# Projection blocks two chunks deep, with exchanged copies taken from the PSUM banks

## The chip, the cores and the metric

The kernel runs on one core of one Trainium2 chip. The metric is the device time of one execution in microseconds (us). A difference of under about 0.2% (6.5 us) can't be told from no change. The engines are called PE (matmul), DVE (vector), ACT (scalar), POOL (GpSimd) and SP (which issues most DMAs).

## The reference

`x` has 4 images of 32 x 32 tokens with 192 channels (4096 tokens). Cut to what matters here, the reference is

```python
x = x + conv_attention(layer_norm(x))     # L0: q, k, v = y @ qkv_w.T + qkv_b, 12 heads of 16
t = t + routed_experts(layer_norm(t))     # 8 experts, top 2
x = x + conv_attention(layer_norm(x))     # L1
h = ln1(layer_norm(t)) ; t = t + attention(h) ; t = t + mlp(t) ; t = t + experts(ln2(t))
```

Each `conv_attention` adds to its scores a bias of relative positions, `einsum(q, Rh)` over rows and `einsum(q, Rw)` over columns. All three attentions begin with the same work: normalize the tokens, then project them to q, k and v with a bias vector.

## The kernel before

`build` (line 2328) runs stages one after the other. The function `front` (line 196) is the projection block. It runs three times: as **c0** (with `load`, it also loads the tokens), as **c1** (with `back`, it first adds the rows that the experts left in DRAM) and as **f1** (with `hidden`, a layer norm within a layer norm, and without relative positions). After each comes `attention` (line 735), which starts when all stores of q, k and of the position bias have landed.

`front` treats the 4096 tokens as 8 chunks of 512 (4 tiles of 128 tokens). Every product is done in float16 with a high and a low part of each operand, so that the sum is close to float32. For one chunk the work is this:

- DVE takes statistics (`prepare`, line 481: in c1 first eight additions at line 491; `bn_stats` at line 506; `spread`, lines 450 to 459), ACT takes the square root (`root`, line 607), and DVE finishes mean and factor (`settle`, lines 466 to 476). c0 and f1 do this for 8 tiles at once, that is in every second chunk; c1 for 4.
- The chunk is normalized into `nrm` (2 buffers): by DVE in c0 (line 521), by ACT in c1 and f1 (line 619).
- PE turns it (`turn_over`, lines 365 and 366) into the banks t0 and t1. ACT writes the high parts (`high_parts`, line 625) and DVE the low parts (`low_parts`, lines 530 and 531). t0 and t1 exist once, so the next `turn_over` waits for `low_parts`.
- PE projects: `turned(c, g)` for g = 0, 1, 2 gives q and k of four heads (6 products of 512 columns, lines 377 to 382, the last is the bias as a product of `cl` with ones) and `values(t)` for four tiles gives v (5 products of 192 columns, lines 389 to 393). Both have three banks in turn (`qp`, `vp`).
- ACT reads a bank into `high` (`high_of`, line 638), then DVE writes `low` (line 540) and, having read `vp` with the bias `bv` added, `vt` (line 543); both stand in `take`.
- SP stores q and k (line 272) once DVE has written `low` for an image and group; in f1 POOL stores the keys.
- In c0 and c1, ACT copies q of a chunk, high and low, with rows and columns of the image exchanged, into `by_x` (`by_column`, line 648): six copies of 64 x 512 float16, one chunk late, read from SBUF with a step of 16 elements. The last chunk's six copies come after the loop.

Each engine has its own order, written out by hand. Before, step c is this, and chunk c-1's projection and chunk c's turning stand in the same step:

```python
for c in range(CHUNKS + 1):               # DVE
    if c: take(c - 1)
    if c < CHUNKS: low_parts(c)
    if c + 1 < CHUNKS: prepare(c + 1); finish(c + 1)
```

PE does `turned(c-1, 0..1)`, `values`, `turn_over(c)`, `turned(c-1, 2)`, `values`. After the chunks, in c0 and c1, PE multiplies q with the tables of positions (lines 435 to 440: 48 units of a bank, 12 products of 128 columns each where k is 0, 8 where k is 1), ACT and DVE drain high and low parts (lines 693 and 597), and ACT and SP store them (line 278). ACT stores a set of eight units while it drains the next set.

In c1 POOL gathers the experts' rows (line 328), eight indirect DMAs a chunk, into four ring buffers.

Of the kernel before, what the change touches and what calls it, by code (L numbers as in the profile page):

```python
# [16 lines left out]
F16 = mybir.dt.float16  # L17
# [7 lines left out]
T = B * L  # L25
# [170 lines left out]
def front(nc, name, src, eps, stats, parts, ident, vt, w, scratch, kept, spare=None, load=None, back=None, hidden=None):  # L196
# [10 lines left out]
    by_act = load is None  # L207
# [3 lines left out]
    with Pool(nc, name) as m:  # L211
# [13 lines left out]
        raw_c, ch, cl = m.sb("rawc", 2 * C, parts=64), m.sb("ch", 2 * C, F16, parts=64), m.sb("cl", 2 * C, F16, parts=64)  # L225
        ones = m.sb("ones", CHUNK, F16, parts=64)
        bv = m.sb("bv", C)
# [8 lines left out]
        s_zero, s_w, s_b, s_tab = m.sem("zero"), m.sem("w"), m.sem("b"), m.sem("tab")  # L236
# [8 lines left out]
        s_byx = m.sem("byx")  # L245
# [8 lines left out]
        by_x = parts  # L254

# [4 lines left out]
        def by_rows(t, c, g):  # L260

            return t[0:GW, at(c, g)].rearrange("p (s y x) -> p s x y", s=2, y=QSIDE)
# [19 lines left out]
        with nc.Block() as block:  # L282
            @block.sync
            def _(sp):
# [13 lines left out]
                sp.dma_start(raw_c[:, :], w["bqk"]).then_inc(s_w, 16)  # L298
                sp.dma_start(bv[:, :], w["bv"].broadcast_to([P, C])).then_inc(s_b, 16)
# [58 lines left out]
            def _(pe):  # L358
# [10 lines left out]
                def turned(c, g):  # L369
# [14 lines left out]
                def values(t):  # L384
# [8 lines left out]
                    pe.matmul(bank, xb[:, tokens], bl[:, 2 * C:W], start=False, stop=True).then_inc(s_v, 1)  # L393
# [3 lines left out]
                for c in range(CHUNKS + 1):  # L397
                    if c == 1:
# [3 lines left out]
                    if c:  # L402
                        for g in range(2):
                            turned(c - 1, g)
                            values(TC * (c - 1) + g)
                    if c < CHUNKS:
                        turn_over(c)
                    if c:
                        turned(c - 1, 2)
                        for j in range(2, TC):  # L410
                            values(TC * (c - 1) + j)
# [7 lines left out]
                for g in range(GROUPS):  # L419
                    top, rest = high[:, g * T:(g + 1) * T], low[:, g * T:(g + 1) * T]  # L420
                    for k in range(2):
                        if k and g == 0:
                            pe.wait_ge(s_byx, 2 * CHUNKS * GROUPS)
# [20 lines left out]
            def _(dve):  # L444
# [65 lines left out]
                def finish(c):  # L510

                    if TC * c % SET == 0:
                        settle(TC * c, SET, mean, rstd, TC * c // SET + sets)
                    if by_act:
                        return
                    dve.wait_ge(s_rstd, 5 * (TC * c // SET + sets + 1))
                    if c >= 2:
                        dve.wait_ge(s_turned, c - 1)
                    for j in range(TC):
                        t = TC * c + j  # L520
                        dve.tensor_scalar(nrm[c % 2][:, j * C:(j + 1) * C], src[:, ts(t, C)], mean[:, t:t + 1],
                                          rstd[:, t:t + 1], ALU.subtract, ALU.mult).then_inc(s_norm, 1)
# [10 lines left out]
                def take(c):  # L533
                    for j in range(TC):
                        t = TC * c + j
                        b, kt = t // KT, t % KT
                        if j < GROUPS:
                            n, cols = c * GROUPS + j, at(c, j)
                            dve.wait_ge(s_hi, n + 1)
                            dve.scalar_tensor_tensor(out=low[:, cols], in0=qp[n % 3][:, :], scalar=1.0 / W_SCALE,  # L540
                                                     in1=high[:, cols], op0=ALU.mult, op1=ALU.subtract).then_inc(s_lo, 1)
                        dve.wait_ge(s_v, t + 1)
                        dve.scalar_tensor_tensor(out=vt4[:, NH // 2 * b:NH // 2 * (b + 1), kt, :],
                                                 in0=vp[t % 3][:, 0:C].rearrange("p (g f) -> p g f", f=2 * HD),
                                                 scalar=1.0 / W_SCALE,
                                                 in1=bv[:, :].rearrange("p (g f) -> p g f", f=2 * HD),
                                                 op0=ALU.mult, op1=ALU.add).then_inc(s_vt, 1)

                def queries_of(t):
                    return t[:, 0:2 * C].rearrange("p (g s f) -> p g s f", g=GROUPS, s=2)[:, :, 0, :]  # L550

# [4 lines left out]
                else:  # L556
                    if load:
                        prepare(0)
                dve.wait_ge(s_w, 7 * 16)
                for t in (raw_a, raw_b, raw_c):  # L560
                    dve.tensor_scalar(queries_of(t), queries_of(t), float(HD) ** -0.5, None, ALU.mult).then_inc(s_q, 1)
                if not load:
                    prepare(0)
                finish(0)
                dve.wait_ge(s_wh, 4)
                for n, (raws, tops, lows) in enumerate(((raw_a[:, :], ah[:, :], al[:, :]),
                                                        (raw_b[0:C1, :], bh[0:C1, :], bl[0:C1, :]),
                                                        (raw_c[32:64, :], ch[32:64, :], cl[32:64, :]))):
                    dve.scalar_tensor_tensor(out=lows, in0=raws, scalar=W_SCALE, in1=tops, op0=ALU.mult,
                                             op1=ALU.subtract).then_inc(s_wl, 1)  # L570
                dve.wait_ge(s_b, 16)
                for c in range(CHUNKS + 1):
                    if c:
                        take(c - 1)
                    if c < CHUNKS:
                        low_parts(c)
                    if c + 1 < CHUNKS:
                        prepare(c + 1)
                        finish(c + 1)
# [21 lines left out]
            def _(act):  # L601
# [7 lines left out]
                def normalize(c):  # L609
                    if TC * c % SET == 0:  # L610
                        root(TC * c, SET, TC * c // SET + sets)
                    if not by_act:
                        return
# [21 lines left out]
                def high_of(c, g):  # L635
# [3 lines left out]
                                   scale=1.0 / W_SCALE).then_inc(s_hi, 1)  # L639

                def by_column(c):

                    act.wait_ge(s_v, TC * (c + 1))
                    act.wait_ge(s_lo, GROUPS * (c + 1))
                    act.wait_ge(s_hi, GROUPS * (c + 1))
                    for g in range(GROUPS):
                        for rows, buf in ((slice(0, GW), high), (slice(GW, P), low)):
# [5 lines left out]
                if load:  # L653
                    root(0, SET, 0)
# [5 lines left out]
                if not load:  # L660
                    normalize(0)
# [1812 lines left out]
```

## Time and profile before

| | |
|---|---|
| median of 3 runs (lowest to highest) | 3267.11 us (3266.5 to 3270.53) |
| profiled execution: device time, span | 3268.62 us, 3266.5 us |
| PE, PEld, DVE, ACT, POOL busy | 81%, 37%, 73%, 59%, 14% of the span |
| mean granted PE clock | 0.90 of full (2.4 GHz) |
| c0: first projection product to first bias product | 24.8 to 114.1 us |
| c1: the same | 1128.5 to 1236.4 us |
| f1: first projection product to last value read | 1925.0 to 2034.1 us |

Read it so: the device time is the span plus some 2 us at its ends. Busy shares are means over stages with different limits. The three projection phases take 306 us of the 3266.5, and it is within them that the change acts. A granted clock of 0.5 is the lower level (1.2 GHz), 1.0 the upper (2.4 GHz); a mean between them is time spent at either.

### The profile page before, as it was taken

The numbers are of one execution on the slowest core, as the hardware profiler recorded it, in microseconds if no ns is written. First come the engines' busy times: TensorE is split into PE (matmuls) and PEld (weight loads), VectorE is DVE, ScalarE is ACT, GpSimd is POOL, SyncE is SP. The second block draws the span as 40 slices with busy tenths as digits, with TensorE's granted clock in tenths as the row PEclk, the third lists the DMA queues.
The fourth block names the chain that finished last, engine by engine and source line by source line (L and its number), as shares of the span: only waits on it lengthen the run. The fifth ranks groups of instructions, "written<-read, shape, count | busy, mean of one in ns | idle before, by whom it ended". The sixth has DMA issues, their size and how long they took to land. (4 is left out here: it accounts for less than half of the span.)

```text
span 3266.5 us, 62245 instructions
## 1 busy us (share of the span) xinstructions
PE 2633.6 (81%) x18588; PEld 1197.2 (37%) x18588; DVE 2399.4 (73%) x4681; ACT 1937.5 (59%) x2701; POOL 455.1 (14%) x542
## 2 busy tenths in 40 slices
PE   5648999997499575599999956488888859599998
PEld 2502222225499434122222233011111336266666
DVE  5578999984665565799999654799999644565565
ACT  5716777773255476277777733177777734564654
POOL 0010111111333440101111101101112100000000
PEclk9859999997599877699999977599999979699999
DMA  2475776663122236656766512112222100200000
GB/s 84 155 152 105 150 149 142 144 143 119 55 76 78 74 101 187 117 124 147 149 146 145 109 39 58 34 52 58 64 60 63 47 22 1 73 6 5 10 9 11
DMA packets 209761, 282.39 MB, mean 86 GB/s; under 512 B 57934, under 2 KB 101886, under 8 KB 209610
## 3 DMA queue, kind: packets, MB, share of 16 engines
q1 hardware_dynamic: 166250, 213.15, 28.7%
q0 software_dynamic: 23696, 34.77, 4.5%
q10 hardware_dynamic: 19664, 32.60, 3.3%
q8 instruction: 77, 1.26, 0.2%
q14 instruction: 74, 0.61, 0.1%
HBM read 201.94 MB, written 77.46 MB: 86 GB/s over the span
## 5 line engine op out<-in xcount | busy, mean ns | idle before, releaser
L988 DVE TENSOR_REDUCE c0att_mx<-c0att_m 128x1 f32<-128x512 f32 x768 | 493.3, 685 | 35.0 <-PE c0att_m L925 29.3
L988 DVE TENSOR_REDUCE c1att_mx<-c1att_m 128x1 f32<-128x512 f32 x768 | 493.3, 685 | 34.8 <-PE c1att_m L925 29.6
L988 DVE TENSOR_REDUCE f1att_mx<-f1att_m 128x1 f32<-128x512 f32 x768 | 480.1, 682 | 21.3 <-PE f1att_m L925 19.3
L1263 ACT ACTIVATE c0att_p<-c0att_s 128x1024 f32<-128x1024 f32 x384 | 373.9, 1020 | 151.7 <-PE c0att_s L941 151.6
L1263 ACT ACTIVATE c1att_p<-c1att_s 128x1024 f32<-128x1024 f32 x384 | 373.9, 1020 | 150.9 <-PE c1att_s L941 150.7
L1263 ACT ACTIVATE f1att_p<-f1att_s 128x1024 f32<-128x1024 f32 x384 | 373.3, 1020 | 121.3 <-PE f1att_s L941 121.3
L925 PE MATMUL f1att_m<-f1att_km,f1att_qm 48*128 48x512 f16 x768 | 156.3, 403 | 130.9 <-DVE f1att_mx L988 99.4
L1694 ACT ACTIVATE moe_h<-moe_u,moe_bu 128x512 f32<-128x512 f32 x192 | 136.7, 712 | 177.0 <-PE moe_u L1611 95.1
L925 PE MATMUL c0att_m<-c0att_km,c0att_qm 64*128 64x512 f16 x768 | 156.4, 403 | 64.6 <-DVE c0att_mx L988 36.2
L925 PE MATMUL c1att_m<-c1att_km,c1att_qm 64*128 64x512 f16 x768 | 156.3, 403 | 62.8 <-DVE c1att_mx L988 35.0
L954 PE MATMUL c1att_o<-c1att_p,c1att_vs 128*32 128x512 f32 x1536 | 206.1, 609 | 0.6 <-ACT c1att_p L1263 0.6
L954 PE MATMUL c0att_o<-c0att_p,c0att_vs 128*32 128x512 f32 x1536 | 206.0, 608 | 0.6 <-ACT c0att_p L1263 0.6
L954 PE MATMUL f1att_o<-f1att_p,f1att_vs 128*32 128x512 f32 x1536 | 205.8, 608 | 0.7 <-ACT f1att_p L1263 0.5
L1624 PE MATMUL moe_y<-moe_dh,xt 128*128 128x192 f16 x1536 | 195.5, 246 | 0.0
L1731 DVE TENSOR_TENSOR xt<-moe_h,xt 128x512 f16<-128x512 f32 x192 | 131.3, 691 | 86.5 <-ACT xt L1696 85.6
L1624 PE MATMUL moe_y<-moe_dl,xt 128*128 128x192 f16 x768 | 189.1, 246 | 0.0
L925 PEld LDWEIGHTS f1att_m<-f1att_km,f1att_qm 48*128 48x128 f16 x768 | 38.1, 93 | 371.2 <-DVE f1att_mx L988 335.1
L925 PEld LDWEIGHTS c0att_m<-c0att_km,c0att_qm 64*128 64x128 f16 x768 | 37.9, 93 | 298.6 <-DVE c0att_mx L988 265.4
L925 PEld LDWEIGHTS c1att_m<-c1att_km,c1att_qm 64*128 64x128 f16 x768 | 37.8, 93 | 297.1 <-DVE c1att_mx L988 264.8
L941 PE MATMUL c0att_s<-xt,c0att_ka 113*128 113x512 f16 x512 | 136.5, 389 | 7.1 <-DMA xt<-c0att_mrow 6.6
L941 PE MATMUL c1att_s<-xt,c1att_ka 113*128 113x512 f16 x512 | 136.5, 389 | 6.9 <-DMA xt<-c1att_mrow 6.3
L1624 PEld LDWEIGHTS moe_y<-moe_dh,xt 128*128 128x128 f16 x1536 | 139.2, 98 | 3.8 <-issue 0.3
(623 smaller groups left out, 5326.3 us busy)
## 6 DMA issues: line engine op xcount, KB each, us to landing
xt<-rel_parts SPq DMA_DIRECT2D x256, 128.0 KB, 5.0
xt<-qk_parts SPq DMA_DIRECT2D x192, 128.0 KB, 4.4
y<-rel_parts SPq DMA_DIRECT2D x128, 128.0 KB, 5.8
y<-qk_parts SPq DMA_DIRECT2D x96, 128.0 KB, 5.3
c0att_qm<-rel_parts SPq DMA_DIRECT2D x144, 64.0 KB, 2.1
c1att_qm<-rel_parts SPq DMA_DIRECT2D x144, 64.0 KB, 2.1
f1att_ka<-qk_parts SPq DMA_DIRECT2D x144, 64.0 KB, 2.1
expert_rows<-y SPq DMA_DIRECT2D x39, 192.0 KB, 2.0
```

Source lines behind the costliest of these rows:

```text
L925: ins = pe.matmul(bank[:, :], qm[v][rows, q0:q0 + P], km[v][rows, c * CHUNK:(c + 1) * CHUNK], start=True, stop=True)
L941: ins = pe.matmul(sps[h][:, c * CHUNK:(c + 1) * CHUNK], ka[u][rows, kcol], qa[u][rows, queries(h, version, c * CHUNK, CHUNK)], start=True, ...
L954: ins = pe.matmul(ops[row:row + 32, :], vs[u][:, (h * KT + kt) * 32:(h * KT + kt + 1) * 32], pr[h][kt % 2][:, c * CHUNK:(c + 1) * CHUNK], ...
L988: dve.tensor_reduce(mx[:, n:n + 1], bank[:, :], AX.X, ALU.max).then_inc(s_mx, 1)
L1263: act.activation(pr[h][kt % 2][:, :], sps[h][:, :], ACT.Exp).then_inc(s_e, 1)
L1624: ins = pe.matmul(yps[q % 2][t // 2][:, (t % 2) * C:(t % 2 + 1) * C], hidden[q % 2][:, x], down[:, w], start=k == 0 and i == 0, stop=k == ...
L1694: act.activation(h32[:, i % 2 * CHUNK:(i % 2 + 1) * CHUNK], bank[:, :], ACT.Gelu, bias=bias, scale=1.0 / W_SCALE).then_inc(s_h32, 1)
L1731: dve.tensor_tensor(hl[q % 2][:, cols], h32[:, i * CHUNK:(i + 1) * CHUNK], hh[q % 2][:, cols], ALU.subtract).then_inc(s_hl, 1)
```

## The change

`front` is rewritten in its order and in a few of its operations:

- **Two steps apart.** The loop has 10 steps. In step s DVE prepares chunk s and ACT normalizes it last in the step; chunk s-1 is turned and split into parts; chunk s-2 is projected and read out. The turning stands behind the first unit `turned(c, 0)`.
- **Roots early.** ACT's `root` comes right after `high_parts`; DVE's `settle` comes after the first `low_of`.
- ACT normalizes in c0 too.
- **Exchanged copies from the banks.** The high half of `by_x` is written by ACT straight from the PSUM bank, right after `high`; the low half by DVE from `low`. The copies of a chunk belong to its own step, and none is left behind the loop. `low_of` and the bank's next use now also wait for ACT's exchanged copy.
- **Bias of v as a product.** `cl` and `raw_c` are 576 wide, `values` has a sixth product (64 rows, 192 columns), `bv` and its DMA are gone. v is read out by ACT in c1 and by DVE in c0 and f1.
- The parts of x lie in `xt` (halves) and no longer in `y` (thirds), which `by_x` keeps for itself.

```diff
@@ front, PE @@
                     if n >= 3:
                         pe.wait_ge(s_lo, n - 2)
+                        if rel:
+                            pe.wait_ge(s_byh, n - 2)
...
-                    pe.matmul(bank, xb[:, tokens], bl[:, 2 * C:W], start=False, stop=True).then_inc(s_v, 1)
+                    pe.matmul(bank, xb[:, tokens], bl[:, 2 * C:W], start=False, stop=False)
+                    pe.matmul(bank, ones[:, 0:P], cl[:, 2 * C:W], start=False, stop=True).then_inc(s_v, 1)
...
+                for step in range(1, CHUNKS + 2):
+                    c = step - 2
...
+                    if c >= 0:
+                        turned(c, 0)
+                    if step <= CHUNKS:
+                        turn_over(step - 1)
+                    if c >= 0:
+                        values(TC * c)
+                        for g in range(1, GROUPS):
+                            turned(c, g)
+                            values(TC * c + g)
+                        values(TC * c + GROUPS)
@@ front, DVE @@
+                def exchange(c, g):
+                    if not rel:
+                        return
+                    dve.wait_ge(s_lo, c * GROUPS + g + 1)
+                    dve.tensor_copy(by_columns(by_x[g][GW:P, :], c), by_rows(low, c, g)).then_inc(s_byl, 1)
...
+                if back:
+                    scale_queries()
+                for step in range(CHUNKS + 2):
+                    c = step - 2
+                    if step < CHUNKS:
+                        prepare(step)
+                    if c >= 0:
+                        low_of(c, 0)
+                    if step < CHUNKS:
+                        finish(step)
+                    if c >= 0:
+                        take(TC * c)
+                    if 1 <= step <= CHUNKS:
+                        low_parts(step - 1)
+                    if c >= 0:
+                        exchange(c, 0)
+                        for g in range(1, GROUPS):
+                            low_of(c, g)
+                            take(TC * c + g)
+                            exchange(c, g)
+                        take(TC * c + GROUPS)
+                    if step == 0 and not back:
+                        scale_queries()
+                    if step == 1:
+                        split_low()
@@ front, ACT @@
+                    if rel:
+                        act.activation(by_columns(by_x[g][0:GW, :], c), exchanged(qp[n % 3][0:GW, :]), ACT.Identity,
+                                       scale=1.0 / W_SCALE).then_inc(s_byh, 1)
...
+                for step in range(CHUNKS + 2):
+                    c = step - 2
+                    if c >= 0:
+                        high_of(c, 0)
+                        take(TC * c)
+                    if 1 <= step <= CHUNKS:
+                        high_parts(step - 1)
+                    if step < CHUNKS and TC * step % SET == 0:
+                        root(TC * step, SET, TC * step // SET + sets)
+                    if c >= 0:
+                        high_of(c, 1)
+                        take(TC * c + 1)
+                        high_of(c, 2)
+                    if step < CHUNKS:
+                        normalize(step)
+                    if c >= 0:
+                        for j in range(2, TC):
+                            take(TC * c + j)
...
-                by_column(CHUNKS - 1)
```

## Rows read from the trace of the kernel before

**Rows 1.** Windows: c0, c1, f1 projection phases, then c0's bias drain; columns named first.

```profile
core 0: us, PE busy (x) PEld busy (x) DVE busy (x) ACT busy (x) POOL busy (x), PEclk, DMA share, GB/s
24.80:114.10 89.30, 68.16 (x360) 34.20 (x361) 54.35 (x159) 64.21 (x82) 0.00 (x0) 0.89 0.16 55
1128.50:1236.40 107.90, 75.93 (x361) 36.03 (x362) 73.06 (x235) 77.00 (x114) 45.61 (x47) 0.81 0.29 90
1925.00:2034.50 109.50, 80.30 (x360) 37.46 (x360) 52.34 (x151) 43.76 (x80) 14.30 (x24) 0.75 0.20 48
126.00:170.00 44.00, 27.07 (x384) 23.77 (x384) 31.51 (x48) 27.74 (x48) 0.00 (x0) 0.85 0.84 261
```

**Rows 2.** Waits (us in total, times, longest): c0's projection phase, then f1's.

```profile
DVE c0qkv_low L540 <- ACT c0qkv_high L638: 30.3, 12, 4.8
PE c0qkv_qp L377 <- DVE y L531: 19.1, 8, 2.9
...
DVE f1qkv_low L540 <- ACT f1qkv_high L638: 55.0, 21, 3.6
```

**Rows 3.** Timeline of DVE, one step of c1: start, us, line, operands, idle before.

```profile
1197.60 2.85 DVE L491 SCALAR_TENSOR_TENSOR x<-c1qkv_sent,top,x 128x192 f32<-128x192 f32 x8
1200.48 1.14 DVE L506 BATCH_NORM_STATS2 stats<-x 128x6 f32<-128x192 f32 x4
1201.65 0.17 DVE L450 TENSOR_TENSOR c1qkv_mean<-stats 128x4 f32<-128x4 f32 x1
...
1202.71 0.18 DVE L466 RECIPROCAL c1qkv_rstd<-c1qkv_std 128x4 f32<-128x4 f32 x1 [0.27 <-ACT c1qkv_std L607]
...
1203.51 0.16 DVE L476 SCALAR_TENSOR_TENSOR c1qkv_away<-c1qkv_mean,c1qkv_rstd 128x4 f32<-128x4 f32 x1
...
1208.78 0.69 DVE L540 SCALAR_TENSOR_TENSOR c1qkv_low<-c1qkv_qp,c1qkv_high 128x512 f16<-128x512 f32 x1 [0.88 <-ACT c1qkv_high L638]
1209.38 0.61 DVE L543 SCALAR_TENSOR_TENSOR vt<-c1qkv_vp,c1qkv_bv 128x192 f32<-128x192 f32 x2
1209.91 0.68 DVE L530 TENSOR_TENSOR y<-c1qkv_t,y 128x512 f16<-128x512 f32 x1
```

**Rows 4.** Timeline of PE in c0: one chunk's work, then the bias products.

```profile
30.92 0.27 PE L365 MATMUL c0qkv_t<-ident,c0qkv_sent 128*128 128x128 f32 x1
...
31.80 0.38 PE L377 MATMUL c0qkv_qp<-y,c0qkv_ah 128*128 128x512 f16 x1
...
32.97 0.39 PE L382 MATMUL c0qkv_qp<-c0qkv_ones,c0qkv_cl 64*128 64x512 f16 x1
33.29 0.26 PE L389 MATMUL c0qkv_vp<-c0qkv_ah,y 128*128 128x192 f16 x1
...
33.71 0.25 PE L389 MATMUL c0qkv_vp<-c0qkv_ah,y 128*128 128x192 f16 x1
...
36.61 0.61 PE L377 MATMUL c0qkv_qp<-y,c0qkv_ah 128*128 128x512 f16 x1 [2.32 <-DVE y L531]
...
114.12 0.22 PE L438 MATMUL c0qkv_qp<-c0qkv_high,c0qkv_th 128*128 128x128 f16 x1 [1.60 <-DVE vt L543]
...
114.28 0.22 PE L438 MATMUL c0qkv_qp<-c0qkv_high,c0qkv_th 128*128 128x128 f16 x1
```

**Rows 5.** Timeline of ACT: end of c0's projections; then c1's normalization.

```profile
124.69 1.11 ACT L648 ACTIVATE y<-c0qkv_low 64x512 f16<-64x512 f16 x1
125.82 1.57 ACT L693 ACTIVATE c0qkv_sent<-c0qkv_qp 128x512 f16<-128x512 f32 x3
...
129.89 0.69 ACTq L278 DMA_DIRECT2D rel_parts<-c0qkv_sent  x1
...
1203.70 1.86 ACT L619 ACTIVATE c1qkv_sent<-x,c1qkv_away,c1qkv_rstd 128x192 f32<-128x192 f32 x4 [1.03 <-DVE c1qkv_away L476]
```

**Rows 6.** Timelines of POOL and DVE in c1: last gather, first additions.

```profile
1187.17 0.95 POOL L328 DMA_INDIRECT c1qkv_sent<-expert_rows,give  x1 [0.30 <-issue]
...
1115.74 2.85 DVE L491 SCALAR_TENSOR_TENSOR x<-c1qkv_sent,top,x 128x192 f32<-128x192 f32 x8 [5.02 <-DMA c1qkv_sent<-expert_rows,give]
```

More of the change, by code:

```diff
@@ new lines, in low_of, with take @@
+                def low_of(c, g):
+                    n, cols = c * GROUPS + g, at(c, g)
+                    dve.wait_ge(s_hi, n + 1)
+                    if rel:
+                        dve.wait_ge(s_byh, n + 1)
+                    dve.scalar_tensor_tensor(out=low[:, cols], in0=qp[n % 3][:, :], scalar=1.0 / W_SCALE,
+                                             in1=high[:, cols], op0=ALU.mult, op1=ALU.subtract).then_inc(s_lo, 1)
+                def take(t):
+                    if back:
+                        return
+                    dve.wait_ge(s_v, t + 1)
+                    dve.tensor_scalar(values_to(t), values_from(t), 1.0 / W_SCALE, None, ALU.mult).then_inc(s_vt, 1)
@@ L555, in _ @@
                     dve.wait_ge(s_rstd, 5)
[L556 to L579, printed above, removed]
+                if back:
+                    scale_queries()
[22 more added lines that the diff above has]
+                        split_low()
                     if rel and c == 1:
@@ L639, in high_of @@
                                    scale=1.0 / W_SCALE).then_inc(s_hi, 1)
[L641 to L647, printed above, removed]
-                            act.activation(by_columns(by_x[g][rows, :], c), by_rows(buf, c, g),
-                                           ACT.Identity).then_inc(s_byx, 1)
+                    if rel:
+                        act.activation(by_columns(by_x[g][0:GW, :], c), exchanged(qp[n % 3][0:GW, :]), ACT.Identity,
+                                       scale=1.0 / W_SCALE).then_inc(s_byh, 1)
@@ L651, in _, with take @@
+                def take(t):
+                    if not back:
+                        return
+                    act.wait_ge(s_v, t + 1)
+                    act.activation(values_to(t), values_from(t), ACT.Identity, scale=1.0 / W_SCALE).then_inc(s_vt, 1)
                 if hidden:
                     root(0, TILES, 0)
-                if load:
-                    root(0, SET, 0)
-                act.wait_ge(s_q, 3)
-                act.activation(ah[:, :], raw_a[:, :], ACT.Identity, scale=W_SCALE).then_inc(s_wh, 1)
@@ L657, in _ @@
[L657 to L673 removed]
+                if back:
+                    split_high()
@@ new lines, in _ @@
+                for step in range(CHUNKS + 2):
[16 more added lines that the diff above has]
+                            take(TC * c + j)
+                    if step == 0 and not back:
+                        split_high()
```

113 lines of the change are left out of this document (40 added, 73 removed).

## The prediction

> **What bounds the kernel now.** I looked first at the windows of the three projection phases [rows 1]. In none of them is an engine full: PE is busy 68.2 of 89.3 us in c0, 75.9 of 107.9 in c1, 80.3 of 109.5 in f1; DVE 54.4, 73.1, 52.3; ACT 64.2, 77.0, 43.8. So a chain bounds them. The waits name it [rows 2]: in c0 DVE waits 30.3 us for ACT's `high` and PE 19.1 us for DVE's low parts; in f1 DVE waits 55.0 us. Line 377's first product of a chunk starts after 2.32 us of idleness and then at the lower clock (0.61 us against 0.38) [rows 4]. Chunk c's read-out, chunk c+1's low parts and its projection stand one behind the other, 11.2 us a chunk in c0, 13.5 in c1 and 13.7 in f1 (by eighths) [rows 1]. The granted clock is 0.89, 0.81 and 0.75: part of PE's busy time is the lower level. Last, in c0 the first bias product is at 114.12 [rows 4], but ACT drains its first bank at 125.82, since its exchanged copies still run at 124.69, 1.11 us each [rows 5]. From there DMA is the limit: 261 GB/s and a share of 0.84 in c0's drain [rows 1].
>
> **Prices, start to start.** PE at the upper clock [rows 4]: `turned` 33.29 - 31.80 = 1.49; `values` 33.71 - 33.29 = 0.42; `turn_over` 31.80 - 30.92 = 0.88. DVE [rows 3]: `low` 1209.38 - 1208.78 = 0.60; a v read-out 0.53 / 2 = 0.27; low parts 2 x 0.7 = 1.4; statistics of 4 tiles 1201.65 - 1200.48 = 1.17; additions 2.88; both chains 1203.67 - 1201.65 less the wait for the root of some 0.3, 1.75. ACT: four normalizations 1.86, three drains of a bank 1.57, one exchanged copy from SBUF some 1.13 [rows 5].
>
> **The new operations.** *Sixth product of v.* Line 382 (64 rows) starts 32.97 and line 389 0.32 later, where a 512-column product takes 0.22; the five before it take 31.80 to 32.97, 1.17 for 5 x 0.215. So a change between 128 and 64 rows costs some 0.1 each way, and the product itself 0.08: I take 0.28 for each of 32 tiles, bounds 0.08 and 0.32. A chunk on PE is then 3 x 1.49 + 4 x 0.70 + 0.88 = 8.15 us at the upper clock, before 7.03.
> *ACT's exchanged copy from the bank.* The drains of line 693 read a bank into float16, 0.5 us start to start [rows 5]; half of all 48 units of that line read with a large step, and the mean of all 48 is the same, 27.74 / 48 = 0.58 us of busy time [rows 1]. I take 0.5, bounds 0.5 and 1.15. ACT's work on a c0 chunk is then 3 x (0.5 + 0.5) + 1.0 + 1.8 = 5.8, below DVE's at either bound.
> *DVE's exchanged copy E from SBUF.* No such DVE copy is in the trace. ACT's copy is the same walk of 64 x 512 float16 at a step of 32 bytes, and takes 1.13 where a bank's read takes 0.5 [rows 5]. It is the nearest row: E = 1.15. Bounds: 0.6 (DVE's `low` of as many columns [rows 3]) and 1.7 (half as much again as ACT).
> The Trainium skill (Advanced Engine Details and Errata, SBUF Cachelines) says that accesses landing on a different 16-byte line each time are penalized; by that rule E is well above 0.6, and the trace agrees for ACT. Against the rule, with E at 0.6, the sum below would come out some 11 us lower. Its next section (PSUM Cachelines) makes the same claim of banks, for matmuls; by it ACT's copy would go to the upper bound, which line 693's mean does not bear out.
>
> **c0.** Chunks pipeline, so the busiest engine sets the pace. DVE from the first projection product (24.8, which stays: the weights' splitting leads to it) to the last `low`: 8 x (3 x 0.60 + 4 x 0.27 + 3 x 1.15) = 50.6; low parts of chunks 1 to 7, 9.8; statistics of chunks 2, 4 and 6 (8 tiles each), 3 x (2.34 + 1.75) = 12.3; tables 1.4. Sum 74.1, plus 1.5 in the last step, where DVE follows PE: 100.4. PE alone would need 8 x 8.15 - 0.9 = 64.3, at a granted 0.9 71.4: it fits, barely. 114.1 to 100.4 is **-14**. The normalizations that leave DVE for ACT (1.2 us a chunk) are in this sum.
>
> **c1.** Per chunk DVE has 2.88 + 1.17 + 1.75 + 1.4 + 1.8 + 3.45 = 12.45 (v goes to ACT): eight are 99.6, with the splitting of weights and tables 103. It starts at 1115.74 [rows 6]. Chunk 1's additions now stand ahead of chunk 0's low parts, and its last gather is issued 48 issues of 1.25 us before 1187.17 [rows 6], near 1127, landing near 1128.5, while DVE is through with chunk 0 at 1121.7: 7 us of new idleness. Gathers come every 10 us and are hidden after that. 1115.7 + 103 + 7 + 2 = 1228 for 1236.4: **-8**.
>
> **f1.** DVE has 52.3 / 8 = 6.5 us a chunk, ACT 43.8 / 8 = 5.5 [rows 1], PE 8.15: PE is the bound. I take a granted clock of 0.9, what c0 has now with more gaps: 8 x 8.15 = 65.2, less 0.9 for the first turning, by 0.9 is 71.5 us from 1925.0: 1996.5 for 2034.5, **-38**. What was waiting is gone since the turning, the parts and the products belong to three chunks. POOL's stores of keys follow each `low` as before and stay idle between.
>
> **The tail of c0 and c1.** Twelve copies of 1.15 leave the way. ACT's first store, which opens the DMA-bound part, comes at 129.89 [rows 5], 15.8 us after the first bias product. Now PE gives the pace of the first eight units: three products take 0.16 (114.12 to 114.28) [rows 4], twelve 0.67, eight units 5.4, and one drain: 6.2. **-9.6** in each, **-19** together. The bytes stored are the same, so the end moves with the start. The last chunk's stores of q and k precede the bias stores by some 5 us and are hidden; before they lay beneath the copies.
>
> **At nothing:** the wider `raw_c` and the missing `bv` DMA (in SP's row of weight loads), ACT's v read-outs in c1 (4 x 0.3, ACT has 3 us of slack a chunk), the wait of `low_of` on ACT's copy (0.5 us, DVE has statistics in between).
>
> **Sum** against the profiled execution: 3268.6 - 14 - 8 - 38 - 19 = 3189.6. The median of the runs shown is 1.5 us below that execution, so I say **3189 us** (-2.4%).
>
> **Rivals.**
> *A, all cheap (0.15).* E is 0.6 and PE stays near the upper level. c0 is then PE's, 3 to 5 us less; c1 gains 7 more; f1 at 0.97 4 to 5. 3173. For it: PE's gaps shrink. Against: ACT's 1.13.
> *B, the gain in c0 and c1 is only the tail (0.17).* E is 1.7: 24 x 0.55 = 13.2 us more in each block, c1 even 4 behind before: 3215. Or PE stays at a mean of 0.75, the value of f1 now: 10.9 us a chunk, c0 -2, f1 -23, c1 -5: 3219.
> *C, slower (0.04).* The stretches run mostly at the lower clock. A chunk is 13.6 us at a mean of 0.6: c0 ends at 132, 18 later, c1 9 later, f1 2 earlier, tails -19 + 8 as the first units slow too: 3282. It decides from a mean of about 0.62. Against: PE is idle less often, and the lowest of the three phases has 0.75 [rows 1].
> *D, nothing moves (0.02).* The blocks' ends are set by stores or by the stage's change, not by the projections. Against: the first store follows the drain within 4 us [rows 5], and DMA's share is 0.16 to 0.29 in the projection phases [rows 1].
>
> **Chances.** The forecast has 0.62, with its own range 3177 to 3204. The range 3168 to 3224 adds A and B. Faster by over 0.2% 0.94, the same (within 0.2%, what a measurement of this kernel can't tell from no change) 0.02, slower 0.04.
>
> **What would show it.** Right: c0's first bias product near 100, c1's near 1228 shifted by c0's gain, f1's phase 71 us at a clock near 0.9; DVE's waits for `high` in f1 nearly gone; ACT's first store 6 us after the first bias product; DVE's copy near 1.15. Wrong: a DVE copy of over 1.6 or under 0.7; f1's clock still 0.75; PE waiting in f1 for normalization or for v's banks.

## The result and the profile after

The changed kernel takes **3181.97 us** (median of four runs, 3178.76 to 3185.25) beside 3266.81 for the kernel before, measured with it: ratio **0.974**, 95% interval 0.9723 to 0.9757. The forecast was 3189, the range 3168 to 3224. The profiled execution, the longest of the four, took 3185.25 us, with a span of 3183.2, 83.3 less than before.

Here are windows of the changed kernel, to be read beside [rows 1]: c0's projection phase, then its bias part up to the attention's load of its weights, the same two of c1, and f1 from its first to its last unit of q and k (a unit is one `turned`; PEld is PE's loading of weights).

```profile
core 0: us, PE busy (x) PEld busy (x) DVE busy (x) ACT busy (x) POOL busy (x), PEclk, DMA share, GB/s
26.90:97.90 71.00, 68.18 (x392) 33.90 (x393) 61.08 (x155) 44.83 (x92) 0.00 (x0) 1.00 0.20 71
97.90:153.40 55.50, 32.46 (x480) 28.25 (x480) 32.80 (x48) 28.66 (x48) 0.00 (x0) 0.84 0.81 252
1113.30:1197.50 84.20, 72.54 (x393) 35.75 (x394) 72.97 (x204) 51.56 (x127) 40.33 (x40) 0.89 0.34 104
1197.50:1257.00 59.50, 32.38 (x480) 28.74 (x480) 33.04 (x49) 28.66 (x48) 0.00 (x0) 0.78 0.79 241
1881.50:1947.70 66.20, 64.48 (x374) 32.27 (x374) 49.84 (x146) 43.52 (x78) 12.33 (x20) 0.97 0.31 73
```

In c0 PE does in 71 us what took it 89, and 32 more products; the granted clock is 1.00 instead of 0.89, in f1 0.97 instead of 0.75. ACT's 64 us have become 45.

The waits of the changed kernel in c0's phase (total, times, longest):

```profile
ACT c0qkv_high L651 <- PE c0qkv_qp L388: 20.7, 16, 4.9
...
DVE c0qkv_low L537 <- ACT y L654: 6.3, 10, 1.1
...
PE c0qkv_qp L383 <- DVE xt L530: 0.8, 2, 0.5
```

and in f1's:

```profile
ACT f1qkv_high L651 <- PE f1qkv_qp L388: 20.6, 15, 4.9
...
DVE f1qkv_low L537 <- ACT f1qkv_high L651: 6.2, 7, 1.5
```

The direction has turned [rows 2]. In c0 DVE waited 30.3 us for ACT and PE 19.1 for the low parts; these are 6.3 and 0.8, and it is ACT that waits. In f1 DVE's 55.0 us have become 6.2. The 6.3 us are `low` waiting for ACT's exchanged copy (L654). Not in these rows is a wait of PE of 12.6 us for `cl`, the weights' low part, which ends with the first projection product, here at 26.9.

DVE's timeline in one step of c0, with the new copy (L550) beside `low` (L537) and v's read-out (L544), in the place of [rows 3]:

```profile
35.99 0.69 DVE L537 SCALAR_TENSOR_TENSOR c0qkv_low<-c0qkv_qp,c0qkv_high 128x512 f16<-128x512 f32 x1
36.59 0.35 DVE L544 TENSOR_SCALAR vt<-c0qkv_vp 128x192 f32<-128x192 f32 x1
36.97 0.62 DVE L550 COPY y<-c0qkv_low 64x512 f16<-64x512 f16 x1
37.63 0.69 DVE L537 SCALAR_TENSOR_TENSOR c0qkv_low<-c0qkv_qp,c0qkv_high 128x512 f16<-128x512 f32 x1
```

The copy takes 0.62 us, not 1.15. The sixth product of v is as priced. On PE's timeline of one `values`, its first product, its fifth and sixth (L400) and the next one's first are

```profile
61.48 0.26 PE L395 MATMUL c0qkv_vp<-c0qkv_ah,xt 128*128 128x192 f16 x1
...
61.82 0.25 PE L399 MATMUL c0qkv_vp<-c0qkv_bl,xt 128*128 128x192 f16 x1
62.00 0.25 PE L400 MATMUL c0qkv_vp<-c0qkv_cl,c0qkv_ones 64*128 64x192 f16 x1
62.18 0.26 PE L395 MATMUL c0qkv_vp<-c0qkv_ah,xt 128*128 128x192 f16 x1
```

62.18 - 61.48 = 0.70, against 0.42 before. The tail is what follows the projections: the bias products, their drains and stores. Its start in c0 is on these rows of the changed kernel (first bias product, ACT's first drain, its first store; before 114.12, 125.82 and 129.89 [rows 4, 5]):

```profile
97.91 0.27 PE L447 MATMUL c0qkv_qp<-c0qkv_high,c0qkv_th 128*128 128x128 f16 x1 [2.04 <-DVE vt L544]
...
99.39 0.60 ACT L712 ACTIVATE c0qkv_sent<-c0qkv_qp 128x512 f16<-128x512 f32 x1 [3.82 <-PE c0qkv_qp L449]
...
105.49 0.69 ACTq L283 DMA_DIRECT2D rel_parts<-c0qkv_sent  x1
```

### The profile page after: what moved, and what is told of

The parts are those of the page before. It is cut to its first block and busy times, and to the rows that moved or that the text cites. A ratio compares the mean times of both kernels' runs of the same rounds, so it can differ in the third digit from the quotient of the medians.

```text
span 3183.2 us, 62491 instructions
## 1 busy us (share of the span) xinstructions
PE 2619.3 (82%) x18684; PEld 1194.0 (38%) x18684; DVE 2413.1 (76%) x4665; ACT 1876.8 (59%) x2717; POOL 456.6 (14%) x542
## 5 line engine op out<-in xcount | busy, mean ns | idle before, releaser
L1007 DVE TENSOR_REDUCE c0att_mx<-c0att_m 128x1 f32<-128x512 f32 x768 | 493.4, 685 | 34.8 <-PE c0att_m L944 29.7
L1007 DVE TENSOR_REDUCE c1att_mx<-c1att_m 128x1 f32<-128x512 f32 x768 | 493.4, 685 | 34.1 <-PE c1att_m L944 28.9
```

What stands on the lines that cost most here:

```text
L1007: dve.tensor_reduce(mx[:, n:n + 1], bank[:, :], AX.X, ALU.max).then_inc(s_mx, 1)
```

## The experiments

All kernels are edits of the changed one. They ran on three chips, each beside the kernel before, which took 3266.3 us on the first (copies_late, one_step, copy_twice, five_v), 3264.2 on the second (rows128, both v_on_act, start_up) and 3265.6 on the third (the others). So medians of different chips can be compared to some 3 us. The ratio is the measurement's own and differs by up to 0.0014 from the quotient of two medians of this table. The places come from one profiled execution each, which can lie far from the median of its kernel: 13.6 us above it in v_on_act_rows128, 12.8 in root_late, 7.6 in turn_second, 5.6 in five_v. In the eleven kernels that leave no copies behind the loop the drain, whose bytes are the same, goes from 55.1 to 62.1, so one execution doesn't show a difference of a few us in one place.

The columns are **c0** from the first product of q and k (L383) to the first bias product; **drain** from there to the first load of the attention's projection weights (`c0att_pw`); **c1 block** from the load of c1's weights (`rawa`) to `c1att_pw`; **f1** from the first to the last unit of q and k.

| kernel | us | ratio (95%) | c0 | drain | c1 block | f1 |
|---|---|---|---|---|---|---|
| before | 3266.8 | 1 | 89.3 | 63.7 | 197.1 | 105.6 |
| changed | 3182.0 | 0.974 (.9723-.9757) | 71.0 | 55.5 | 177.8 | 66.2 |
| copies_late | 3266.4 | 1.0002 (.999-1.0014) | 115.1 | 62.4 | 214.7 | 66.1 |
| copies_behind | 3218.1 | 0.9854 (.9838-.9871) | 85.8 | 64.1 | 193.9 | 66.2 |
| one_step | 3281.5 | 1.0051 (1.0034-1.0068) | 108.2 | 55.1 | 199.0 | 104.8 |
| copy_twice | 3194.9 | 0.9794 (.9772-.9817) | 78.1 | 55.4 | 182.7 | 66.5 |
| five_v | 3175.3 | 0.9731 (.9713-.9748) | 70.8 | 56.8 | 178.7 | 65.8 |
| rows128 | 3176.2 | 0.9728 (.9712-.9744) | 67.3 | 57.6 | 178.1 | 64.6 |
| v_on_act | 3176.7 | 0.9729 (.9713-.9745) | 67.6 | 57.6 | 176.5 | 66.9 |
| v_on_act_rows128 | 3172.5 | 0.9716 (.9699-.9732) | 63.4 | 62.1 | 179.2 | 65.0 |
| start_up | 3179.5 | 0.9733 (.9716-.9749) | 71.4 | 56.8 | 180.2 | 65.9 |
| root_late | 3201.2 | 0.9792 (.9772-.9813) | 83.7 | 55.9 | 184.8 | 73.4 |
| turn_second | 3205.1 | 0.9812 (.9795-.9828) | 79.4 | 58.3 | 178.1 | 82.8 |
| straight | 3174.4 | 0.9716 (.97-.9732) | 68.9 | 57.2 | 174.3 | 66.0 |

### Is the miss the size of DVE's copy?

copy_twice:

```diff
                     dve.wait_ge(s_lo, c * GROUPS + g + 1)
+                    dve.tensor_copy(again[GW:P, :].rearrange("p (s x y) -> p s x y", s=2, x=QSIDE), by_rows(low, c, g))
                     dve.tensor_copy(by_columns(by_x[g][GW:P, :], c), by_rows(low, c, g)).then_inc(s_byl, 1)
```

> The changed kernel with DVE's exchanged copy made twice (the second into a buffer of its own), so that the pair costs about the 1.15 us that the prediction gave to one. Theory (the prediction's sum failed only by the size of this copy): DVE then has 61 + 15 = 76 us of work in c0's phase of 71 and 73 + 15 = 88 in c1's of 84; the first bias product of c0 goes from 97.9 to 102 to 106 and c1's phase from 84 to 92 to 98. Together +12 to +22, 3194 to 3204 us, and f1 as it is. Rival (the copies are hidden at either size, the miss has another cause): within 4 us of the changed kernel, 3178 to 3186.

3194.94, 13 us above the changed kernel and clear of noise, with c0 7.1 and c1's block 4.9 longer and f1 as it was: the theory, though c1's phase, at 91.0, stayed just under the 92 to 98. A pair of copies costs 1.23, so with E near 1.15 this kernel would have come within some 6 us of the forecast, from above.

straight:

```diff
-                    dve.tensor_copy(by_columns(by_x[g][GW:P, :], c), by_rows(low, c, g)).then_inc(s_byl, 1)
+                    dve.tensor_copy(by_x[g][GW:P, c * CHUNK:(c + 1) * CHUNK], low[0:GW, at(c, g)]).then_inc(s_byl, 1)
...
-                        act.activation(by_columns(by_x[g][0:GW, :], c), exchanged(qp[n % 3][0:GW, :]), ACT.Identity,
+                        act.activation(by_x[g][0:GW, c * CHUNK:(c + 1) * CHUNK], qp[n % 3][0:GW, :], ACT.Identity,
```

> The changed kernel with the two exchanged copies made straight: DVE's from SBUF and ACT's from the bank read their 512 elements in order, so that half of the bias inputs are in the wrong order and this part of the result is left wrong. It measures what the 32-byte step costs each engine. If the step costs DVE nothing, as its 0.616 us beside the 0.69 of a low from a bank suggest, the straight copy stays at 0.6 and the time within 2 us. If the step does slow DVE (the rule of the Trainium skill, Advanced Engine Details and Errata, SBUF Cachelines, which ACT's 1.11 to 1.13 us bore out), the straight copy is well below, 0.2 to 0.4 us, and c0's phase is 1 to 4 us shorter, c1's 4 to 8: 3170 to 3178 us. ACT's copy from the bank stays at 0.58 by either.

The instructions of the two lines in this kernel (min/median/max ns), DVE's from SBUF, then ACT's from a bank:

```profile
L550 DVE COPY y<-c0qkv_low x24: 277/287/289, 32.9 to 92.9; 64x512 f16<-64x512 f16 x24
```

```profile
L654 ACT ACTIVATE y<-c0qkv_qp x24: 577/578/579, 28.3 to 91.2; 64x512 f16<-64x512 f32 x24
```

and the same two in the changed kernel:

```profile
L550 DVE COPY y<-c0qkv_low x24: 602/617/636, 35.4 to 96.7; 64x512 f16<-64x512 f16 x24
```

```profile
L654 ACT ACTIVATE y<-c0qkv_qp x24: 577/578/579, 30.2 to 95.0; 64x512 f16<-64x512 f32 x24
```

The step makes DVE's copy 2.15 times as long, and costs ACT's read of a bank nothing. The prediction's error was to carry ACT's time over: DVE is slowed too, but from 0.287. The kernel's 3174.4 lies in the range, but its interval still overlaps that of the changed kernel, and c1's phase is 2.2 shorter, where 4 to 8 were expected. The Trainium skill (VectorE: DVE Perf Modes, What auto-detection actually checks) gives DVE its fastest mode only where a single source and the destination lie in SBUF, both 16-bit at a step of one. That the strided copy is the slower one agrees with this; which mode either copy ran in is not shown.

### Does the order need the early copies, or the copies the order?

copies_late:

```diff
+                def by_column(c):
+                    act.wait_ge(s_lo, GROUPS * (c + 1))
+                    act.wait_ge(s_hi, GROUPS * (c + 1))
+                    for g in range(GROUPS):
+                        for rows, buf in ((slice(0, GW), high), (slice(GW, P), low)):
+                            act.activation(by_columns(by_x[g][rows, :], c), by_rows(buf, c, g),
+                                           ACT.Identity).then_inc(s_byh, 1)
...
                         high_of(c, 2)
+                    if rel and c > 0:
+                        by_column(c - 1)
                     if step < CHUNKS:
                         normalize(step)
```

> The changed kernel with its new order, but the exchanged copies as before: all six by ACT from SBUF, one chunk late, the last chunk's behind the projections. Theory (the order needs the cheap copies): ACT then has 3 x 0.5 + 6 x 1.13 + 1.0 + 1.9 = 11.2 us of work in each chunk of c0, more than the 8.7 PE needs, and becomes the bound there: c0's first bias product near 115 instead of 97.9, c1's phase some 14 us longer than 84.1, both tails 8 to 10 us longer; f1, which has no such copies, stays at 69. Together about +50, 3232 us. Rival (the copies only cost the two tails, since ACT hides them in the steps): c0's first bias product stays within 2 us of 97.9, and the time is about +19, 3201 us.

3266.4, 34 us above the theory and not to be told from the kernel before. f1 keeps its whole gain (66.1), and c0 is 26 us longer than before the change, its first bias product at 140.0 where the theory had 115. Its window and its waits in c0's phase:

```profile
24.90:140.00 115.10, 80.75 (x392) 39.42 (x392) 46.79 (x131) 75.36 (x107) 0.00 (x0) 0.82 0.13 42
```

```profile
DVE c0qkv_low L532 <- ACT c0qkv_high L643: 56.2, 21, 9.1
PEld c0qkv_t L369 <- ACT c0qkv_sent L624: 33.4, 5, 6.7
ACT c0qkv_high L643 <- PE c0qkv_qp L386: 32.3, 16, 4.9
PE c0qkv_t L369 <- ACT c0qkv_sent L624: 31.9, 5, 6.4
```

ACT is busy 75 of 115 us, so its work is not the bound. PE's turning waits 31.9 us for the normalization, which stands behind six copies; meanwhile ACT waits 32.3 for PE. They take turns, which neither theory nor rival had.

copies_behind changes only that place:

```diff
-                    if rel and c > 0:
-                        by_column(c - 1)
                     if step < CHUNKS:
                         normalize(step)
+                    if rel and c > 0:
+                        by_column(c - 1)
```

> The kernel of the run copies_late (new order, exchanged copies by ACT from SBUF, one chunk late), with one thing moved: in a step ACT now normalizes ahead of the six copies, not behind them. Theory (what cost 44 us in c0's phase there was not only ACT's work but its place: the copies stood between the last read-out of a chunk and the normalization that PE's turning waits for, so PE and ACT took turns): ACT's work of 11.2 us a chunk remains the bound, c0's phase 88 to 95 instead of 115.1, c1's 98 to 105 instead of 122.8, total 3220 to 3235 us against 3266. Rival (the copies delay ACT's high as well, which frees the banks, so the place does not matter): within 8 us of 3266.

```profile
24.90:110.70 85.80, 74.39 (x393) 36.19 (x394) 46.38 (x131) 74.16 (x106) 0.00 (x0) 0.90 0.17 57
```

3218.1, 48 us faster for two lines swapped, and 2 below the range. c0 is at 85.8, where 88 was the least expected, and ACT (74.2) and PE (74.4, at a granted 0.90) are now busy alike, so that ACT alone is the bound isn't shown. This kernel and the changed one differ by the copies' engine, source and time, and by the waits that belong to them, so early cheap copies are worth 3218.1 - 3182.0 = 36 us in the new order; which of the three counts was not tried. In the profiled executions c0 has 14.8 of it, its drain 8.6 and c1's block 16.1.

one_step:

```diff
+                for c in range(CHUNKS + 1):
+                    if c:
+                        for g in range(GROUPS):
+                            low_of(c - 1, g)
+                            take(TC * (c - 1) + g)
+                            exchange(c - 1, g)
+                        take(TC * (c - 1) + GROUPS)
+                    if c < CHUNKS:
+                        low_parts(c)
+                    if c + 1 < CHUNKS:
+                        prepare(c + 1)
+                        finish(c + 1)
```

(DVE's loop; PE's and ACT's likewise in the order of before, the normalization of c0 left on ACT.)

> The changed kernel with its new copies and the bias product of v, but the order of before: chunk c's read-outs ahead of chunk c+1's low parts on DVE, turning behind the second unit, roots beside the normalization (which stays on ACT in all three blocks, as do c1's v read-outs). Theory (the distance of two steps makes the projection phases, the copies make the tails): f1's phase goes back to about 109 us (+40), c0's to 84 to 89 (+13 to +18), c1's by +8 to +12; the tails stay at 7 to 8 us. Sum +61 to +70, 3243 to 3252 us. Rival (in c0 and c1 it was ACT's copies out of the way that shortened the chain, not the distance): only f1 goes back, 3222 us.

3281.54, 15 us slower than the kernel before, and 30 more than expected. f1 goes back to 104.8: its gain is the order's alone, and the sixth product costs nothing there. The drain stays at 55.1: its gain is the copies' alone. c0's phase is 19 us worse than before, c1's 8 (116.1 for 107.9). The waits in c0's:

```profile
DVE c0qkv_low L536 <- ACT y L647: 42.8, 19, 4.2
ACT c0qkv_high L644 <- PE c0qkv_qp L388: 35.6, 17, 5.2
PE c0qkv_qp L383 <- DVE xt L529: 25.5, 8, 3.7
```

In the old order read-outs, low parts and the next projection are one chain, and every early copy is a link of it: `low` waits for ACT's copy, the low parts stand behind DVE's. So in c0's projection phase the copies alone lose 19 us and the order alone gains 3.5 at best (copies_behind, 85.8 for 89.3), where the two together gain 18. (Part of the 19 may be the normalization that moved to ACT; that wasn't tried alone.)

### Early root, and turning behind the first unit

root_late:

```diff
-                    if step < CHUNKS and TC * step % SET == 0:
-                        root(TC * step, SET, TC * step // SET + sets)
                     if c >= 0:
                         high_of(c, 1)
                         take(TC * c + 1)
                         high_of(c, 2)
+                    if step < CHUNKS and TC * step % SET == 0:
+                        root(TC * step, SET, TC * step // SET + sets)
```

> The changed kernel with one thing undone: ACT takes the root behind the third high of a step, beside the normalization, not behind the high parts. DVE waits for it in the middle of the statistics' chain, in order, with v's read-out, the low parts and the later lows behind it. Theory (the early root is part of what makes the pipeline): DVE waits some 3 to 5 us more in each step with a root, 3 such steps of c0 and f1 and 7 of c1: c0's phase +8 to +15, f1's +8 to +15, c1's +15 to +30; total +30 to +60, 3212 to 3242 us. Rival (DVE has the slack, 10 us in c0 and 16 in f1): under +8, 3190 us at most.

turn_second:

```diff
                     if c >= 0:
                         values(TC * c)
-                        for g in range(1, GROUPS):
-                            turned(c, g)
-                            values(TC * c + g)
+                        turned(c, 1)
+                        values(TC * c + 1)
+                    if step <= CHUNKS:
+                        turn_over(step - 1)
+                    if c >= 0:
+                        turned(c, 2)
+                        values(TC * c + 2)
```

> The changed kernel with the turning on PE behind the second unit of a step, as before, not behind the first. ACT's high parts and DVE's low parts of that chunk come 2.2 us later, and DVE stands in wait for them with the second low behind it. Theory (PE and DVE are balanced at 8.7 us a chunk, so a wait of DVE in each of 7 steps shows): c0's and f1's phases +7 to +14 each, c1 +0 to +7, total +14 to +35, 3196 to 3217 us. Rival (the three banks and DVE's slack cover it): within 4 us of 3182.

root_late costs 19 us by the medians, less than the 30 to 60 expected. Its profiled execution lies 12.8 above its median, so its places are rather too large: c0 12.7 longer as foreseen, f1 7.2, just under its 8, c1's block only 7.0, far under 15 to 30. Its waits in c0's phase carry a row that is 1.2 us in the changed kernel:

```profile
DVE c0qkv_rstd L475 <- ACT c0qkv_std L624: 10.2, 3, 6.3
```

turn_second costs 23 us, within the range; f1 suffers most (+16.6, over the 14 expected), c0 8.4, c1's block 0.3. Again a wait that is small in the changed kernel (0.8 us) has come:

```profile
ACT xt L648 <- PE c0qkv_t L370: 21.6, 7, 4.3
```

Both places count in c0 and f1. In c1 the turning's place doesn't, which fits gathers and DVE's additions setting the pace there; start_up, below, bears on that.

### What bounds the projection phases now?

five_v leaves v's bias out of the result:

```diff
-                    pe.matmul(bank, xb[:, tokens], bl[:, 2 * C:W], start=False, stop=False)
-                    pe.matmul(bank, ones[:, 0:P], cl[:, 2 * C:W], start=False, stop=True).then_inc(s_v, 1)
+                    pe.matmul(bank, xb[:, tokens], bl[:, 2 * C:W], start=False, stop=True).then_inc(s_v, 1)
```

> The changed kernel without v's sixth product, so v's bias is left out. Theory (c0 and f1 are bound by PE): 32 x 0.28 = 9.0 us less in each of these two phases, first bias product of c0 near 89 instead of 97.9, f1's phase near 60; c1, where DVE and the gathers set the pace, 0 to 2 less. 3162 to 3164 us. Rival (DVE, busy 61 of 71 us in c0, takes over at once): c0 gains under 4 and f1 9, about 3170. Rival (the product is hidden, as its cover is waits): 3182, within 3 us of the changed kernel.

rows128:

```diff
-        raw_c, ch, cl = m.sb("rawc", W, parts=64), m.sb("ch", W, F16, parts=64), m.sb("cl", W, F16, parts=64)
-        ones = m.sb("ones", CHUNK, F16, parts=64)
+        raw_c, ch, cl = m.sb("rawc", W, parts=64), m.sb("ch", W, F16, parts=64), m.sb("cl", W, F16)
+        ones = m.sb("ones", CHUNK, F16)
...
+                pool.memset(cl[64:P, :], 0.0).then_inc(s_zero, 1)
```

> The changed kernel with the bias products on 128 rows: cl and ones have 128 partitions, cl's rows 64 to 127 are zero, so PE no longer changes between 128 and 64 rows (0.2 us for each of 56 products in a block: 24 of q and k, 32 of v). That takes 11 us of PE's work out of each projection phase. Theory (after the run with five products: PE and DVE are balanced, what PE saves it waits for v's banks and for low parts, and partly gives back at the lower clock): c0's and f1's phases at most 2 us shorter each, 3174 to 3180 us. Rival (PE's switches are what the row-64 product costs, and they stall PE where nothing else does): -8 to -11 in c0 and f1 each, 3162 us.

five_v takes 9 us from PE's work (32 x 0.28), and both phases stay (70.8 for 71.0, 65.8 for 66.2): my theory that PE alone bounds them fell. c0's first bias product is at 95.6, not near 89; of the 2.3 us that it comes earlier, 2.0 are the later start of the changed kernel's execution. PE's timeline in five_v shows the saving run out (start, us, line, idle before):

```profile
67.64 0.26 PE L395 MATMUL c0qkv_vp<-c0qkv_ah,xt 128*128 128x192 f16 x1 [1.40 <-DVE vt L543]
...
68.95 0.61 PE L383 MATMUL c0qkv_qp<-xt,c0qkv_ah 128*128 128x512 f16 x1 [0.72 <-DVE xt L529]
69.35 0.63 PE L384 MATMUL c0qkv_qp<-xt,c0qkv_al 128*128 128x512 f16 x1
```

and the windows of five_v after that wait, and of the changed kernel over the same microseconds:

```profile
69.00:78.00 9.00, 9.00 (x36) 4.50 (x36) 7.23 (x14) 3.93 (x8) 0.00 (x0) 0.65 0.26 94
```

```profile
69.00:78.00 9.00, 8.43 (x52) 4.26 (x51) 8.64 (x21) 6.89 (x14) 0.00 (x0) 1.00 0.26 101
```

PE waits for DVE, which has come out of the eight tiles' statistics, and then does 36 products in 9 us at a granted 0.65 where the changed kernel does 52, of other lengths in part, at 1.00. So in c0 PE and DVE are balanced (68.2 and 61.1 of 71 us busy): time taken from one turns into waiting for the other, here also into the lower level. In f1 the granted clock falls from 0.97 to 0.92. rows128 says the same: PE's busy time in c0 falls from 68 to 59 us, its phase by 3.7, f1's by 1.6 (at most 2 each were expected).

v_on_act (`take` on ACT in all three blocks):

```diff
-                    if not back:
-                        return
                     act.wait_ge(s_v, t + 1)
```

> The changed kernel with all v read-outs on ACT, in c0 and f1 as in c1. DVE loses 11.2 us of work in each of these phases (61 to 50 in c0, 50 to 39 in f1), ACT, which waits 20 us for PE in each, gains about as much. Theory (PE and DVE are balanced): PE's own work, 68.2 us in c0 and 64.5 in f1, is left, so c0's phase goes from 71.0 to 68 to 69 and f1's from 66.2 to 65; together -3 to -4, 3178 to 3179 us. Rival (PE alone is the bound): no change, within 2 us. Rival (ACT's chain high, copy, low is what matters, and v's read-outs get in its way): +5 to +10.

> Both at once: v's read-outs on ACT and the bias products on 128 rows. Theory (balance of PE and DVE): now both engines have 11 us less, so c0's phase falls from 71.0 to 59 to 62 and f1's from 66.2 to 55 to 58, c1 within 2 us; about -20, 3160 to 3164 us, far more than the sum of the two alone (-4 to -8). Rival (a third thing sets the 8.7 us of a chunk, the chain PE, ACT, DVE through three banks): less than 10 us gained, over 3172.

v_on_act: c0 67.6, with PE busy 67.0 of it; f1 66.9, no gain. Both edits at once, c0's and then its waits in f1's phase:

```profile
24.70:88.10 63.40, 57.00 (x393) 36.99 (x394) 52.10 (x123) 50.71 (x124) 0.00 (x0) 1.00 0.20 73
```

```profile
DVE f_parts L531 <- ACT f_parts L644: 13.4, 4, 4.2
...
PE f1qkv_qp L385 <- DVE f_parts L532: 8.4, 7, 2.6
```

In the changed kernel f1's wait of DVE for the parts is 7.4 us, not 13.4. c0 falls by 7.6, about the sum of the two alone (3.7 and 3.4), not far more; f1 by only 1.2. In f1 what is left is the path of a chunk's parts: ACT's four activations on them, then DVE's low parts, then PE. The rival of a third bound holds there, with 3172.5 in all against the 3160 to 3164 I expected. Of c0's earlier end (first bias product 88.1 for 97.9) only 3.2 us reach `c0att_pw` (150.2 for 153.4): the drain is 62.1 instead of 55.5. Why it is longer when it begins earlier is open: from 100 to 115 us its DMA share is only 0.77, where the changed kernel has 0.94 to 0.96 for 30 us. This profiled execution took 3186.2, 13.6 over its kernel's median, so the places above don't show where the median's gain lies. The kernel has the lowest median of all that compute the whole result, 0.3% under the changed one, but the intervals overlap, and a gain over it is not shown.

start_up:

```diff
+                    if step == 1 and back:
+                        low_parts(0)
                     if step < CHUNKS:
                         prepare(step)
+                    if step == 1 and not back:
+                        split_low()
```

(In c1 `split_low` stands at the end of step 0.)

> The changed kernel with the weights' low parts split before chunk 0's low parts (in c1 also ahead of chunk 1's additions), and in c1 chunk 0's low parts ahead of chunk 1's additions, which wait 6.2 us for a gather. Theory (the later first product is pure delay): first projection product of c0 at 25 instead of 26.9, of c1 25 to 28 us after the block's start instead of 34.1; the gathers still set c1's pace from there, so of those 6 to 9 us 0 to 6 arrive: 3173 to 3180 us. Rival (hidden: c1's end is set by DVE's work and the gathers whatever comes first): within 2 us in c1, 3180 us.

c1's first product comes at 24.8 us of the block instead of 34.1, yet the first bias product stays at 118.3 us of it, and the block is 2.4 longer: the rival. The third additions (chunk 2's) show why. In the changed kernel they begin at 1114.27, 35.1 us into the block, with 1.07 us of idleness; here they begin 34.8 us into it:

```profile
1111.71 2.85 DVE L500 SCALAR_TENSOR_TENSOR x<-c1qkv_sent,top,x 128x192 f32<-128x192 f32 x8 [3.99 <-DMA c1qkv_sent<-expert_rows,give]
```

The work moved forward only uncovers the next gather. In f1, which has no gathers, the same edit brings the attention's load 2.3 us nearer to the block's start (100.7 for 103.0).

## Why the prediction was right, and which step of it failed

- **The size of E failed.** The step is "E = 1.15", carried over from ACT's row. Measured: 0.617, which is by the prediction's own list (a copy under 0.7) a sign of being wrong. "E is well above 0.6" failed with it: the copy is slowed, 2.15 times, and still ends at 0.617. The forecast's 7 us too many are less than the 13 that copy_twice adds, so other terms erred the other way. Rival A's conditions were the ones met: E at 0.6, and PE near the upper level (1.00 in c0, 0.97 in f1). Its 3173 is 9 us too few, and more than half of that are the tails (-19 for a measured -13), which it shares with the forecast.
- **c0, -14:** the first bias product came at 97.9, not 100.4 (-16.2). "The busiest engine sets the pace" with DVE at 74.1 was wrong as to the engine: DVE has 61.1, PE 68.2 of 71.0. The first projection product, said to stay at 24.8, was 26.9 here. In nine of the ten experiments that keep the order of the splitting it is 24.7 to 25.1, so the delay comes and goes with the execution.
- **c1, -8:** first bias product 132.8 us after the block's start before, 118.3 now, -14.5: under-priced, as 24 copies were too dear by 0.53 each (12.8 us). With that corrected the sum would give -21, so some 6 us are missing on the other side. It isn't the later first product (34.1 us into the block for 24.9): start_up takes it back and gains nothing. What it is stays open. The idleness of 7 us for gather 1 was real: 6.22 before the additions.

```profile
1103.58 2.85 DVE L500 SCALAR_TENSOR_TENSOR x<-c1qkv_sent,top,x 128x192 f32<-128x192 f32 x8 [6.22 <-DMA c1qkv_sent<-expert_rows,give]
```

- **The tails, -9.6 each:** over-priced. The first store comes 7.6 us after the first bias product in c0 (predicted 6.2; before 15.8) and 6.2 in c1 (before 16.2), and the drains shorten by 8.2 and 4.8. "The end moves with the start" holds in c0 and not in c1, where 10.0 us of earlier stores give 4.8. What takes the rest there wasn't tried, and c1's drain, 59.5 here, goes from 57.6 to 62.6 in the experiments that leave no copies behind the loop.
- **f1, -38:** -40.1 from the block's start to the attention's. Its clock is 0.97, not 0.9. "PE is the bound" fell with five_v: with 9 us less of its work the phase stays. The size was near because PE's 64.3 us at the measured 0.97 come to 66.3; as the phase was no shorter with less work for PE, this is luck in part. one_step shows the new order to be the whole of the gain. It undoes three things at once, the distance of two steps, the early root and the turning's place; alone, the last two cost 7.2 (root_late) and 16.6 (turn_second), the distance wasn't tried alone.
- **The sum:** c0 with its tail -24.4 (predicted -23.6), c1 with its -19.2 (-17.6), f1 -40.1 (-38). In c0 and c1 phases priced too small and tails priced too large cancelled: the totals were better than the terms, and that was luck.
- **v's sixth product:** 0.28 each, as priced, but mostly hidden: five_v's 6.7 us in the median are within the overlap of the intervals.
- **At nothing:** the wait of `low_of` on ACT's copy was put at nothing; it is 6.3 us in c0, in 10 waits of up to 1.1. What it costs the phase wasn't tried.
- **What the prediction did not see:** it priced order and copies apart and added them. The runs of one part alone, 3281.5 and 3218.1 (or 3266.4 by one place), show that they don't add: the copies alone lose 15 us, the order alone gains 49 (or nothing, by one place), together they gain 85. Rival C's outcome, slower, is where the copies alone did end.

## What to carry to other kernels

Before adding up the gains of two parts, ask what each does alone to the chain: an operation put into a chain costs its length (one_step, c0 19 us longer than before), the same one put beside it little. Where two engines are within about a tenth of each other, as PE and DVE were in c0 (68 and 61 of 71 us), most of the work taken from one comes back as a wait, and it can come back as a lower granted clock too (0.65 in five_v's stretch; in c0 of v_on_act_rows128 it stayed at 1.00). Taking from both gave the sum of the two gains, not more. The price of an access pattern belongs to an engine and its source: measure it there, and don't carry it over from another engine.

## What the runs showed of the hardware that I had not expected

A DVE copy of 64 x 512 float16 within SBUF takes 0.287 us in order and 0.617 at a step of 32 bytes. ACT takes 1.11 to 1.13 for that walk from SBUF, where it reads 576 float32 in order from SBUF in 0.67 (the weights' high parts, line 657 of the kernel before), but 0.578 from a bank, with the exchange or without. So in this kernel the strided read was cheapest for ACT straight from the bank. The Trainium skill (Advanced Engine Details and Errata, SBUF Cachelines) foresees a penalty in SBUF where each access falls on another line of 16 bytes, and both engines' numbers agree; how much of DVE's is that and how much a lost mode these runs don't separate. On PE a bias product on 64 rows among products on 128 costs more than its columns. From v's fifth product to the first product behind the sixth it is 0.36 us in the changed kernel (61.82 to 62.18) and 0.17 in rows128 (60.85 to 61.02), where the sixth has 128 rows. Widened with zero rows to 128, the 56 such products took 9.6 us less of PE's busy time in c0.
